# The mask products of S on 64 rows each, in two row halves, placed ahead of the next tile's transposition

## What is computed

```python
x = L0_attn_x
x = x + 0.5 * _L0_ffn_ref(_layernorm(x), ...)     # six layers of attention and MLP
x = x + _L0_attn_ref(_layernorm(x), ...)          # linear recurrence
x = x + 0.5 * _L0_ffn_ref(_layernorm(x), ...)     # the same six layers again

# in a layer: 16 heads of 64, window 32; every window sees itself and the one before
q = l2norm(q) * qs;  k = l2norm(k) * ksc          # then rotary embedding
bk2, bv2 = (look(bk), look(bv))
mask = (it < jb) | (it > jb + w) | (jb == -1)
sim = jnp.einsum('bhwie,bhwje->bhwij', bq, bk2) * QK_SCALE
sim = jnp.where(mask, -jnp.finfo(sim.dtype).max, sim)
attn = jax.nn.softmax(sim, -1)
out = jnp.einsum('bhwij,bhwje->bhwie', attn, bv2)
x = attn_layer(shift_tokens(x), ...) + x          # out @ Wo
x = ffn_layer(shift_tokens(x), ...) + x           # a * gelu(gate) @ W2, behind a layer norm
```

## Time and profile before

| | |
|---|---|
| median of 3 runs | 3624.75 us (3624.67 to 3629.21) |
| the profiled execution | 3626.41 us |
| its span, first to last instruction | 3624.3 us |
| mean granted clock of TensorE | 0.989 |
| PE busy | 3365.4 us, 93% |
| PEld busy | 2479.2 us, 68% |
| DVE busy | 2779.5 us, 77% |
| ACT busy | 2422.0 us, 67% |
| POOL busy | 2185.4 us, 60% |
| mask products (L499) busy on PE | 72.9 us in 192 records |
| products of S (L507) busy on PE | 389.7 us in 24576 records |

### The profile page before, as it was taken

The page is one execution under the profiler, slowest core; times in us unless marked ns, Lnnn a source line. Parts: engine busy times, 40 slices in busy tenths (PEclk is TensorE's granted clock), DMA queues, the critical chain, the costliest instruction groups (busy, mean ns, idle before and its releaser), DMA issues. The chain is left out here.

```text
span 3624.3 us, 164641 instructions
## 1 busy us (share of the span) xinstructions
PE 3365.4 (93%) x63298; PEld 2479.2 (68%) x63490; DVE 2779.5 (77%) x6886; ACT 2422.0 (67%) x3751; POOL 2185.4 (60%) x1383
## 2 busy tenths in 40 slices
PE   2899999999999999999959999999999999999997
PEld 1577777777777777777736677777777777777776
DVE  2677877787877777778668787777787888778875
ACT  0567677777777776777616677777667777677775
POOL 2566666666666666666526666666666666666663
PEclk9999999999999999999979999999999999999998
DMA  3111111111111111111111111111111111111111
GB/s 99 32 47 42 46 45 42 45 43 48 44 46 42 45 43 46 45 43 45 49 36 43 43 45 46 42 46 43 45 45 43 45 42 46 43 48 43 46 43 55
DMA packets 202618, 165.45 MB, mean 46 GB/s; under 512 B 145401, under 2 KB 175229, under 8 KB 201981
## 3 DMA queue, kind: packets, MB, share of 16 engines
q1 hardware_dynamic: 193584, 160.31, 16.1%
q10 hardware_dynamic: 8909, 3.23, 0.4%
HBM read 35.48 MB, written 2.10 MB: 10 GB/s over the span
## 5 line engine op out<-in xcount | busy, mean ns | idle before, releaser
L1065 POOL TENSOR_TENSOR rot<-rot,swp 128x1024 f32<-128x1024 f32 x384 | 907.1, 2362 | 225.8 <-DVE rot L869 225.8
L470 PE MATMUL proj<-wq,xsT 128*128 (+1 forms) x1536 | 807.2, 637 | 111.9 <-ACT xsT L743 43.9
L673 ACT ACTIVATE sq<-proj 128x512 f32<-128x512 f32 x768 | 437.9, 596 | 566.4 <-PE proj L470 564.8
L1074 POOL TENSOR_TENSOR rot<-rot,rn 128x1024 f32<-128x1024 f32 x384 | 722.4, 1903 | 0.0
L1055 POOL TENSOR_TENSOR rt<-rt,half 128x1 f32<-128x1 f32 x192 | 105.3, 549 | 968.3 <-DVE rt L891 968.3
L863 DVE TENSOR_TENSOR swp<-proj,tab 128x512 f32<-128x512 f32 x768 | 524.0, 682 | 185.5 <-ACT sq L673 141.8
L944 DVE SCALAR_TENSOR_TENSOR hT<-proj,b1c,fg 114x128 f32<-114x128 f32 (+1 forms) x576 | 166.6, 345 | 468.4 <-ACT fg L737 460.9
L869 DVE TENSOR_TENSOR rot<-proj,tab 128x512 f32<-128x512 f32 x768 | 517.6, 674 | 3.3 <-PE tps L481 3.3
L470 PEld LDWEIGHTS proj<-wq,xsT 128*128 128x128 f32 x1536 | 248.2, 190 | 390.6 <-issue 341.0
L481 PEld LDWEIGHTS tps<-idf,rot 128*128 128x128 f32 x3072 | 361.5, 141 | 207.6 <-issue 203.5
L1059 POOL TENSOR_TENSOR prob<-prob,rr 128x1024 f32<-128x1024 f32 x192 | 365.3, 1903 | 184.3 <-DVE rr L903 184.3
(11 more groups left out here) (103 smaller groups left out, 5604.7 us busy)
## 6 DMA issues: line engine op xcount, KB each, us to landing
vb<-va SPq DMA_DIRECT2D x192, 384.0 KB, 3.5
vb<-va SPq DMA_DIRECT2D x192, 128.0 KB, 3.4
wq<-in_L_ffn_Wqkv SPq DMA_DIRECT2D x95, 192.0 KB, 2.4
xs<-Z SPq DMA_DIRECT2D x384, 32.0 KB
xs<-Z SPq DMA_DIRECT2D x384, 28.0 KB
xs<-Z SPq DMA_DIRECT2D x384, 3.8 KB
xs<-Z SPq DMA_DIRECT2D x384, 0.2 KB
wo<-in_L_ffn_Wo SPq DMA_DIRECT2D x94, 64.0 KB, 1.9
```

The source lines that it names most:

```text
L470: mm(proj[:, c % 2, :], xsT[:, k.parity(L_QKV), :], wq2[:, bass.ds(w + c * 512, 512)], start=True, stop=True).then_inc(p_qkv[c], 1)
L673: fn(sq[:, c * 512:(c + 1) * 512], proj[:, c % 2, :], ACT.Square).then_inc(a_sq[c], 1)
L1065: g_.tensor_tensor(r, r, swp[:, g * INNER:(g + 1) * INNER], ALU.add).then_inc(g_add[g], 1)
L1074: g_.tensor_tensor(r, r, rn[:, g * HEADS:(g + 1) * HEADS].unsqueeze(2) .to_broadcast([P, HEADS, DH]), ALU.mult).then_inc(g_nm[g], 1)
```

## The change

The two mask products leave `scores` and become `masks`. Each has 64 rows of contraction instead of 128: the first uses the stationary and moving rows 0 to 63, the second rows 64 to 127, so they take different row halves of the array; they write different banks of sps as before. For that the stationary matrix is no longer the identity. It is a constant `spread` which sends a row of the mask to all the output rows with the same place in a window and the same half of the rows, and the mask's rows are laid out anew; the results are the same sums. `spread` is loaded into oT at the start on ScalarE's queue and cast to bf16 into idb, behind the wait for all constants.

The order of TensorE's step changes too. Before: xs transposition, hidden(1), hidden(0), waits (v_sub, v_rs, a_qT, a_kT, a_car), masks, S. After: hidden(1), the same waits, masks, xs transposition, hidden(0), S.

```diff
--- before.py
+++ after.py
@@ -44,7 +44,7 @@
 
 
 def macaron(nc, x_in, w_in, b_in, a_in, b_gain, w_out, b_out, w_qkv, q_scale, k_scale, w_o,
-            ln_g, ln_b, w_1, b_1, w_2, b_2, c_rope, c_mask, c_ident, x2_dram, out):
+            ln_g, ln_b, w_1, b_1, w_2, b_2, c_rope, c_mask, c_ident, c_spread, x2_dram, out):
     with ExitStack() as ctx:
         def sb(name, shape, dt=F32):
             return ctx.enter_context(nc.sbuf_tensor(name, [P] + shape, dt))
@@ -310,7 +310,7 @@
             consts.append((scl[:, 0:DEPTH, kind, :], src.partition_broadcast(P)))
         consts += [
             (prob[:, :, :, :].rearrange("p a b c -> p (a b c)"), c_mask),
-            (boB[:, :], b_out.partition_broadcast(P)),
+            (boB[:, :], b_out.partition_broadcast(P)), (oT[:, 0, :], c_spread),
             (winT[:, :], w_in), (woutT[:, :], w_out),
             (cols[:, 0:1], b_in.rearrange("(p a) -> p a", a=1)),
             (cols[:, 1:2], a_in.rearrange("(p a) -> p a", a=1)),
@@ -491,12 +491,17 @@
                               xnT[:, :], start=True, stop=True, skip_group_check=True)
                 last.then_inc(p_f[a], 1)
 
+            def masks(k):
+
+                first = k.off("first", L_S, lambda u: ((POS - 1 - u % POS) // (POS - 1)) * 512)
+                rows = (slice(0, DH), slice(DH, P))
+                mm(sps[:, 0, :], idb[rows[0], :], mask[rows[0], bass.ds(first, 512)], start=True, stop=False,
+                   skip_group_check=True)
+                mm(sps[:, 1, :], idb[rows[1], :], mask[rows[1], 0:512], start=True, stop=False, skip_group_check=True)
+
             def scores(k):
-                first = k.off("first", L_S, lambda u: ((POS - 1 - u % POS) // (POS - 1)) * 512)
+
                 par = k.parity(L_S)
-                for ty in range(2):
-                    m = mask[:, bass.ds(first, 512)] if ty == 0 else mask[:, 0:512]
-                    mm(sps[:, ty, :], idb[:, :], m, start=True, stop=False, skip_group_check=True)
                 for p in range(PAIRS):
                     for g in range(2):
                         for hp, ty in ((0, 0), (1, 1), (0, 1), (1, 0)):
@@ -590,24 +595,28 @@
                 if k.on(L_S):
                     k.wait(v_ab[2], L_QKV)
                     values(k, 0)
+                if k.on(L_F):
+                    k.wait(a_xnT, L_F)
+                    k.wait(a_v[1], L_S)
+                    hidden(k, 1)
+                if k.on(L_S):
+
+                    k.wait(v_sub, L_S + 1)
+                    k.wait(v_rs, L_QKV, per=RS_STEPS)
+                    k.wait(a_qT, L_S)
+                    k.wait(a_kT, L_S)
+                    if k.parity(L_S) == 0:
+                        k.wait_even(a_car, L_S)
+                    masks(k)
                 if k.on(L_X):
                     k.wait_pair(d_xs, L_X, 64)
                     k.wait(a_kT, L_S)
                     k.wait(a_pT, L_SM)
                     tr(tps[:, 4, :], xs[:, k.parity(L_X), :], idf[:, :]).then_inc(p_xT, 1)
                 if k.on(L_F):
-                    k.wait(a_xnT, L_F)
-                    for a in (1, 0):
-                        k.wait(a_v[a], L_S)
-                        hidden(k, a)
+                    k.wait(a_v[0], L_S)
+                    hidden(k, 0)
                 if k.on(L_S):
-
-                    k.wait(v_sub, L_S + 1)
-                    k.wait(v_rs, L_QKV, per=RS_STEPS)
-                    k.wait(a_qT, L_S)
-                    k.wait(a_kT, L_S)
-                    if k.parity(L_S) == 0:
-                        k.wait_even(a_car, L_S)
                     scores(k)
 
             def prepare():
@@ -756,9 +765,8 @@
 
             for dst, src in consts:
                 act.dma_start(dst, src).then_inc(d_const, 16)
-            act.wait_ge(d_id, 16)
-            cp(idb[:, :], idf[:, :]).then_inc(s_idb, 1)
             act.wait_ge(d_const, 16 * len(consts))
+            cp(idb[:, :], oT[:, 0, :]).then_inc(s_idb, 1)
             cp(mask[:, :], prob[:, :, :, :].rearrange("p a b c -> p (a b c)")).then_inc(s_mask, 1)
             act.wait_ge(v_z, TILES)
             act.wait_ge(c_zero, 1)
@@ -1132,12 +1140,13 @@
     rope = kinds.reshape(4, POS, P, DH).transpose(2, 0, 1, 3).reshape(P, 4 * POS * DH).astype(f)
 
     row = np.arange(P)
-    i, g = (row % WIN)[:, None], (row // (2 * WIN))[:, None]
+    i, g, low = (row % WIN)[:, None], (row % (2 * WIN) // WIN)[:, None], (row < 2 * WIN)[:, None]
     j = (np.arange(512) % (2 * WIN))[None, :]
     usual = ((j < WIN) & (j >= i)) | ((j >= WIN) & (j - WIN <= i))
-    first = np.where(g == 0, usual & (j >= WIN), usual)
+    first = np.where((g == 0) & low, usual & (j >= WIN), usual)
     mask = np.concatenate([np.where(m, 0.0, NEG) for m in (usual, first)], 1).astype(f)
-    return {"rope": rope, "mask": mask, "ident": np.eye(P, dtype=f)}
+    spread = ((i == i.T) & (g == (row // (2 * WIN))[None, :])).astype(f)
+    return {"rope": rope, "mask": mask, "ident": np.eye(P, dtype=f), "spread": spread}
 
 
 def kernel(**inputs):
```

More of the change, by code:

```diff
@@ L592, in step @@
                     values(k, 0)
-                if k.on(L_X):
-                    k.wait_pair(d_xs, L_X, 64)
-                    k.wait(a_kT, L_S)
-                    k.wait(a_pT, L_SM)
-                    tr(tps[:, 4, :], xs[:, k.parity(L_X), :], idf[:, :]).then_inc(p_xT, 1)
                 if k.on(L_F):
                     k.wait(a_xnT, L_F)
-                    for a in (1, 0):
-                        k.wait(a_v[a], L_S)
-                        hidden(k, a)
+                    k.wait(a_v[1], L_S)
+                    hidden(k, 1)
                 if k.on(L_S):
@@ L610, in step @@
                         k.wait_even(a_car, L_S)
+                    masks(k)
+                if k.on(L_X):
+                    k.wait_pair(d_xs, L_X, 64)
+                    k.wait(a_kT, L_S)
+                    k.wait(a_pT, L_SM)
+                    tr(tps[:, 4, :], xs[:, k.parity(L_X), :], idf[:, :]).then_inc(p_xT, 1)
+                if k.on(L_F):
+                    k.wait(a_v[0], L_S)
+                    hidden(k, 0)
+                if k.on(L_S):
                     scores(k)
```

## The result

| | before | after |
|---|---|---|
| median of the runs | 3624.71 us | 3743.78 us |
| ratio, 95% interval | | 1.0326 (1.0309 to 1.0344) |
| the profiled execution, its span | 3626.41, 3624.3 us | 3741.9, 3740.1 us |

The account below looks back on a forecast made before the run. A loop through rn, masks, S, VectorE's maximum mx and the norms was taken to bound the kernel. The longer step from mask load to S, less spare time, costs 0.61 us a tile on 180 tiles: +110 us, 3735 us; range 3680 to 3785.

Parts of the forecast that it names:

- What bounds: TensorE's masks wait for rn in a loop through S, mx and the norms; work between rn and S is paid.
- The step to S: From first mask load to first product of S: 1.27 us after the change, from 0.62 or 0.55 before.
- load to transposition: From first mask load to the xs transposition, overlapping masks, change of rows and register instruction: 0.38 us, not 0.34.
- transposition to hidden(0): From the xs transposition to the first hidden(0) product on TensorE: 0.15 us, near the usual 0.11.
- the rival of serial masks: The two mask products don't overlap: 0.21 us more on 180 tiles, 38 us, 3773 us; chance 0.08.
- The change of rows at 0.10: On TensorE, switching between products on 128 rows and on half of them adds 0.10 us.
- S's spare time: Between S's end and mx, S could end 0.15 us later for free on one of the two unrolled steps.
- The sign that was to confirm the path: On VectorE, mx would wait for S in nearly every tile if the forecast was right.
- Moves that cost nothing: hidden(1) moves ahead, gelu and hT up to 0.11 us earlier, not counted; later xs transposition and hidden(0) aren't needed sooner.
- TensorE is the bound after all: Only TensorE's stretch from xs transposition to S counts, 2.11 to 1.94 us: 32 us faster, 3593 us; chance 0.06.
- The loop gives way: VectorE's gap ahead of the first rotation absorbs half the loss, 3680 us, chance 0.07; nearly all, chance 0.03.
- the clock falls: TensorE's idle time ahead of the masks lowers its granted clock: some 330 us more, 4070 us; chance 0.02.

Follow-up runs that it names:

- e1: Changed kernel's order of the step, but with the earlier mask products (identity, 128 rows each, one after the other): 3753.7 us.
- e4: Kernel before, with four small VectorE instructions added ahead of the last step that writes rn: 3780.6 us.
- e5: Changed kernel, with VectorE's addition of the MLP's output to Z moved from the middle of the norms to behind rn: 3654.4 us.
- e11: Changed kernel, with four small VectorE instructions added behind bn_stats, between mx and the first rotation: 3744.6 us.
- e7: Changed kernel, but with hidden(0) back ahead of the masks, so only the xs transposition stands behind them: 3646.4 us.
- e10: Kernel before, with the scratch of the norms moved from sps to SBUF and the masks not waiting for rn: 3752.0 us.
- e3: Changed kernel, with the scratch of the norms moved from sps to SBUF and the masks not waiting for rn: 3726.9 us.
- e2: Masks on 64 rows each as in the changed kernel, but in the old place directly ahead of S: 3596.8 us.
- e8: Changed kernel, but with the xs transposition back ahead of hidden(1) and the masks, so only hidden(0) stands behind them: 3728.5 us.

## Why the prediction was right, and where it was off

*What bounds.* Right, for the part from rn to S. rn held the mask loads in the kernel before, although no row named it: the same 0.40 and 0.53 in before, after, e1, e4, e5, and in e4 the delay was paid. The sequencer's register instructions behind the wait were the sign.

*The step to S.* 1.24 against the 1.27 worked out. By terms: load to transposition 0.33 (0.38 was taken, so its waits run in the shadow of the masks, and the low value held); transposition to hidden(0) 0.16 (0.15); hidden(0) to S in all 0.75 (0.74). The 0.15 was right by luck: it was taken as 0.11 and a rest of hidden(0)'s wait, but in e1, with the same wait and no change of rows, the distance is 0.11, so the 0.05 belongs to the way back to 128 rows. The masks overlap in full, starting within 0.01 of each other, so the rival of serial masks fell. The change of rows at 0.10 holds in both directions for the product right behind it, and in e1 one of them is missing, with its 0.10; the 0.05 more on the way back to 128 rows has no term in the forecast.

*S's spare time.* This is the step that failed. The forecast took 0.15 off on tiles like A, since mx started that much later than S allowed. mx was not on the loop; the projection is, and it starts 0.11 behind S's end on tiles like A and 0.49 on tiles like B, before and after the change (medians). So nothing was to spare. The step grew by 0.62 and 0.70, in the mean 0.66, and the tile by 0.67 (17.78 to 18.45). The measured 119 us are that on 178 tiles, against the 180 counted. Without the false term, and with the step at 1.24, the forecast would have been 119. With it, and 0.03 too much in the step, it was 110. The sign that was to confirm the path, mx waiting for S in nearly every tile, came true (38 tiles of the stretch) and proves nothing: mx was merely late behind an S that had become late, and e11 shows that the loop doesn't pass through it.

*Moves that cost nothing.* hT ended earlier relative to mx and didn't matter, as said: mx starts 0.50 behind it, waiting for S. That the xs transposition in its old place fills a wait of hidden(0) for ScalarE's copy was missed. It makes no difference in the changed kernel, where hidden(0) stands behind rn and its first load comes 1.04 and 1.27 behind the copy's end, but it is what e7 is above its range for.

*TensorE is the bound after all.* Refuted for this kernel, but its sum was nearly right as a conditional: 32 us faster if the masks need not wait, and e10 against e3 gives 25, at the price of the slower norms in both.

*The loop gives way; the clock falls.* Neither happened. VectorE's gap ahead of the first rotation is the tail of the squares, so it moves with S and absorbs nothing. The granted clock stays at 1.00, the level of 2.4 GHz (the figure behind the five busy times):

```profile
1000.00:1700.00 700.00, 653.54 (x12535) 480.55 (x12536) 542.08 (x1329) 478.27 (x741) 428.19 (x266) 1.00 0.16 43
```

The 3.3% are thus 0.66 a tile: what hidden(0), the transposition and the added changes of rows put between rn and S, less the 0.21 that the overlap of the masks saves there.

## What to carry to other kernels

Before moving work in an in-order engine's program, ask on which side of its latest wait it stands. Work ahead of a late wait is free up to the wait's end, work behind it is not, and an engine that is 93% busy can still be the one that waits; a distance between releaser and released that is the same in every iteration gives the wait away where no row shows idle time. To find the loop's path, don't stop at the first consumer of a result (mx): compare each consumer's distance in two kernels, and delay one by a known amount. When a change has two parts, run them alone: here one of them, the row halves, was worth 0.77% alone, and 0.94% with a small reordering on VectorE, while the whole cost 3.3%.

## What the runs showed of the hardware

- Two products of 64 rows and 512 columns in different row halves and banks start within 0.01 of each other (after, e2), and what follows on 128 rows starts 0.32 behind them. On 128 rows the same two start 0.22 apart and the next follows after 0.22 (e1). So a change between full and half rows delays the next product by 0.10. On the way back to 128 rows the one after that is late too: hidden(0) comes 0.16 behind the transposition instead of 0.11 (after, e1), S 0.26 instead of 0.20 (e7), and six products of hidden(0) take 0.91 instead of 0.82 (e8).
- Register arithmetic of TensorE's sequencer that stands between a late semaphore and the weight load comes on top of the wait. From rn's end to the load it is 0.40 with three such instructions and 0.53 with four (after, B); ahead of values(0) in e3, with one, it is 0.15 from the rotation's end (1002.50 to 1002.64). This is read from the traces; no run took the arithmetic away.
- Small VectorE instructions (128 x 32) take 0.18 to 0.19 each with one operand in PSUM. With both in SBUF beside a running GpSimd product, one took 2.26 (e3). With one SBUF input and an SBUF output, four of them took 0.42 in e11, where no GpSimd instruction runs beside them, but 0.80 to 0.98 in e4. There two of the four take 0.28 to 0.46 and end within 0.04 of the end of a GpSimd instruction, in the second tile at 1024.09 and 1024.52 against 1024.05 and 1024.49.
